# A product-key stage whose short lists move to PSUM and whose dense output is multiplied a quarter at a time

## The reference, cut to what matters

```python
q = (hidden_states @ Wq).reshape(b, t, 2, H, RET // 2)           # H = 4 heads
sim = jnp.einsum('btphn,hkpn->pbthk', q, keys)                   # 2 sides x 64 keys
sc, ix = jax.lax.top_k(sim, KPH)                                 # the 8 best of each side
all_sc = (sx[..., :, None] + sy[..., None, :]).reshape(b, t, H, KPH * KPH)
scores, pk = jax.lax.top_k(all_sc, KPH)                          # the 8 best of the 64 sums
w = silu(hidden_states . down_embed[idx]) * softmax(scores)
experts_states = sum over heads and k of w * up_embed[idx]
mlp = jax.nn.silu(hidden_states @ Wg + bg) * (hidden_states @ Wu + bu) @ Wd + bd
return mlp + experts_states
```

## Time and profile before

| | |
|---|---|
| median of 3 runs | 1288.74 us (1287.62 to 1289.69) |
| the profiled execution: its time | 1287.9 us |
| its span (first to last instruction) | 1286.1 us |
| mean granted clock of PE | 0.914 |
| busy: PE, DVE, ACT, POOL | 80%, 73%, 48%, 28% of the span |
| this stage | about 608 to 923 us of the span |

### The profile page before, as it was taken

One profiled execution on the slowest core, in us unless ns is written; L12 is line 12 of the kernel. 1 busy time (PEld: TensorE's weight loads), 2 busy tenths in 40 slices (PEclk: granted clock), 3 DMA queues, 4 the chain that ended last, 5 costly groups with the idle time before them and its releaser, 6 DMA issues.

```text
span 1286.1 us, 21270 instructions
## 1 busy us (share of the span) xinstructions
PE 1024.6 (80%) x7331; PEld 662.8 (52%) x7331; DVE 943.0 (73%) x2271; ACT 616.2 (48%) x958; POOL 361.8 (28%) x339
## 2 busy tenths in 40 slices
PE   5868500878969987996598888897879969999998
PEld 3653200844547753553166565576645446666665
DVE  4686699778866666777798889887468856666666
ACT  3424566366622336652565556664276523333332
POOL 5600000011200024451887788775002100000000
PEclk8889955989989999999599889998999979999999
DMA  7000000100000000000000000000000000000000
GB/s 261 1 1 1 1 0 0 59 4 2 2 2 1 0 1 1 2 1 1 1 1 1 1 0 0 0 0 1 1 2 2 2 1 9 9 8 8 8 9 17
DMA packets 8956, 13.47 MB, mean 10 GB/s; under 512 B 816, under 2 KB 6704, under 8 KB 8624
## 3 DMA queue, kind: packets, MB, share of 16 engines
q1 hardware_dynamic: 8880, 12.46, 2.8%
HBM read 10.36 MB, written 2.10 MB: 10 GB/s over the span
## 4 chain that ended last, share of the span: by engine, by line
PE 45%; DVE 34%; issue 12%; ACT 6%; POOL 2%; DVEq 1%; DMA 0%; SPq 0%; POOLq 0%; ACTq 0%
DVE big L718 6%; DVE big L713 6%; PE psum L1879 5%; PE psum L511 5%; PE psum L1882 5%; PE psum L1893 5%; PE psum L1574 3%; DVE big L1785 2%; PE psum L1366 2%; PE psum L1319 2%; DVE tmp L1750 2%; PE psum L1328 2%; ACT psum L1642 2%; PE psum L252 2%; DVE amax L1129 2%
## 5 line engine op out<-in xcount | busy, mean ns | idle before, releaser
L713 DVE TENSOR_REDUCE big<-psum 128x16 f32<-128x1024 f32 x96 | 114.4, 1221 | 70.9 <-PE psum L465 38.0
L1699 POOL TENSOR_TENSOR big<-big 128x512 f32<-128x512 f32 x128 | 134.7, 1086 | 19.9 <-ACT big L1622 19.9
L1929 ACT ACTIVATE big<-psum 128x512 f32<-128x512 f32 x80 | 47.8, 598 | 143.3 <-PE psum L1879 143.1
L1642 ACT ACTIVATE psum<-big,tmp 128x512 f32<-128x512 f32 x128 | 84.9, 687 | 37.2 <-DVE big L1785 33.3
L383 POOL TENSOR_TENSOR big<-big,w_const 128x256 f32<-128x256 f32 x48 | 34.7, 724 | 229.8 <-PE psum L511 216.0
L1785 DVE SCALAR_TENSOR_TENSOR big<-big,tmp,psum 128x512 f32<-128x512 f32 x128 | 90.3, 743 | 4.8 <-ACT psum L1642 1.8
L1709 POOL TENSOR_TENSOR big<-big 128x1024 f32<-128x1024 f32 x32 | 75.4, 2366 | 64.0 <-DVE big L1785 64.0
L1982 DVE TENSOR_TENSOR big<-big,psum 128x512 f32<-128x512 f32 x80 | 54.4, 687 | 53.1 <-PE psum L1882 52.9
L718 DVE RECIPROCAL big<-psum 128x256 f32<-128x256 f32 x48 | 83.9, 1749 | 11.8 <-PE psum L511 11.8
L1893 PEld LDWEIGHTS psum<-tmp,big 128*128 128x128 f32 x512 | 66.7, 191 | 40.0 <-issue 36.3
L619 ACT ACTIVATE big<-psum 128x1024 f32<-128x1024 f32 x64 | 62.0, 1021 | 51.3 <-PE psum L495 51.3
(11 more groups left out here) (239 smaller groups left out, 2391.2 us busy)
## 6 DMA issues: line engine op xcount, KB each, us to landing
out<-X SPq DMA_DIRECT2D x8, 256.0 KB, 2.3
tmp<-in_pack_f SPq DMA_DIRECT2D x1, 1924.0 KB, 7.8
w_f<-in_pack_f SPq DMA_DIRECT2D x1, 1280.0 KB, 12.3
tmp<-in_pack_once SPq DMA_DIRECT2D x1, 960.0 KB, 7.5
X<-in_x SPq DMA_DIRECT2D x1, 768.0 KB, 5.3
w_a<-in_pack_a SPq DMA_DIRECT2D x3, 256.0 KB, 7.6
w_a<-in_pack_a SPq DMA_DIRECT2D x1, 704.0 KB, 9.7
w_f<-in_pack_f SPq DMA_DIRECT2D x1, 576.0 KB, 5.0
```

Of the source, the lines that this page charges most:

```text
L713: dve.tensor_reduce(nm, psum[:, 1 + 2 * t:3 + 2 * t, :].rearrange("p c (r l k) -> p (c r) l k", r=2, k=SK), AX.X, ALU.max, negate=True).th ...
L1642: act.activation(bank(EX_BANK + h % 2), ssum[t][:, h * 512:(h + 1) * 512], ACT.Exp, bias=shift2[:, t * NH2 + h:t * NH2 + h + 1]).then_inc( ...
L1699: ins = pool.tensor_tensor(ssum[t][:, h * 512:(h + 1) * 512].rearrange("p (i j) -> p i j", i=ROWS2), st[:, 0, h, 0:ROWS2].unsqueeze(2).to_ ...
```

## The change

The dense output is split in four calls `dense_out(g, c)`, one quarter of the contraction each: quarters 0 and 1 follow the up product of c = 2 and 3, quarters 2 and 3 the transposes of group g+2. `total(g)` moves from behind the gates into them (after c = 1) and is two instructions instead of three. One of the two lists of eight (`top2y`), the eight best sums (`lead2`) and the sum of the weights (`tot2`) are put in PSUM banks 1 and 2, which the exponentials use later. ACT copies `lead2` to SBUF (`best2`) for the threshold that `weigh` reads, and DVE waits for that copy before the first `weigh`.

```diff
-        top2 = small(GT * 8 * 8).rearrange("p (t c k) -> p t c k", t=GT, c=8)
+        top2x = small(GT * 4 * 8).rearrange("p (t c k) -> p t c k", t=GT, c=4)
...
+        top2y = bank(1)[:, 0:128].rearrange("p (t c k) -> p t c k", t=GT, c=4)
+        lead2 = bank(2)[:, 0:128].rearrange("p (t h k) -> p t h k", t=GT, h=NH2)
+        tot2 = bank(2)[:, 128:128 + GT]
...
+            def dense_out(g, c):
+
+                if c == 0:
+                    pe.wait_ge(sem(s, "res"), at(s, "res") + g + 1)
+                pe.wait_ge(S("f2_aT"), 4 * g + c + 1 + 1)
+                for t in range(GT):
+                    pe.matmul(bank(7)[:, t * P:(t + 1) * P], aT[:, c, t * P:(t + 1) * P],
+                              W["f2_wd"][:, c * P:(c + 1) * P], start=(t == 0 and c == 0), stop=False,
+                              skip_group_check=True)
...
+                    if c >= 2:
+                        dense_out(g, c - 2)
                 if two_more:
                     T(g + 2, j)
-                pe.wait_ge(sem(s, "res"), at(s, "res") + g + 1)
-                pe.wait_ge(S("f2_aT"), 4 * g + 4 + 1)
-                for t in range(GT):
-                    for c in range(4):
-                        pe.matmul(bank(7)[:, t * P:(t + 1) * P], aT[:, c, t * P:(t + 1) * P],
...
+                dense_out(g, 2)
+                dense_out(g, 3)
 
                 def turn_weights(t):
 
-                    pe.wait_ge(S("f2_tt"), 3 * g + 3)
+                    pe.wait_ge(S("f2_tt"), 2 * g + 2)
...
+                if not (isinstance(G, int) and G == 0):
+                    act.wait_ge(S("f2_mw"), 16 * G)
+                act.activation(best2, lead2, ACT.Copy).then_inc(S("f2_b2"), 1)
...
             def top(G, t):
 
                 dve.wait_ge(S("f2_sim"), 4 * G + t + 1 + 2)
+                if t == 0 and not (isinstance(G, int) and G == 0):
+                    dve.wait_ge(S("f2_mw"), 16 * G)
                 settle(dve)
                 for c in range(8):
-                    dve.max(top2[:, t, c, :], sim[:, t * 512 + c * 64:t * 512 + (c + 1) * 64])\
+                    dve.max(top2x[:, t, c, :] if c < 4 else top2y[:, t, c - 4, :], sim[:, t * 512 + c * 64:t * 512 + (c + 1) * 64])\
                         .then_inc(S("f2_t1"), 1)
                 dve.wait_ge(S("f2_t1"), 32 * G + 8 * t + 8)
                 dve.tensor_tensor(pair2[:, t].rearrange("p h (a b) -> p h a b", a=8),
-                                  top2[:, t, 0:4, :].unsqueeze(3).to_broadcast([P, NH2, 8, 8]),
-                                  top2[:, t, 4:8, :].unsqueeze(2).to_broadcast([P, NH2, 8, 8]), ALU.add)\
+                                  top2x[:, t, :, :].unsqueeze(3).to_broadcast([P, NH2, 8, 8]),
+                                  top2y[:, t, :, :].unsqueeze(2).to_broadcast([P, NH2, 8, 8]), ALU.add)\
                     .then_inc(S("f2_t2"), 1)
...
                 for h in range(NH2):
-                    dve.max(best2[:, t, h, :], pair2[:, t, h, :]).then_inc(S("f2_t3"), 1)
+                    dve.max(lead2[:, t, h, :], pair2[:, t, h, :]).then_inc(S("f2_t3"), 1)
...
-                dve.tensor_tensor(e8, best2, best2[:, :, :, 0:1].to_broadcast([P, GT, NH2, 8]), ALU.subtract)\
+                dve.tensor_tensor(e8, lead2, pair2[:, :, :, 0:1].to_broadcast([P, GT, NH2, 8]), ALU.subtract)\
...
-                dve.scalar_tensor_tensor(out=shift2.rearrange("p (t h) -> p t h", t=GT), in0=best2[:, :, :, 0],
+                dve.scalar_tensor_tensor(out=shift2.rearrange("p (t h) -> p t h", t=GT), in0=lead2[:, :, :, 0],
...
             def weigh(G, t):
 
+                if t == 0:
+                    dve.wait_ge(S("f2_b2"), G + 1)
                 for h in range(NH2):
...
-                                             accum_out=tots2[:, t * NH2 + h:t * NH2 + h + 1])\
+                                             accum_out=tots2[:, t, h:h + 1])\
...
-                dve.tensor_reduce(tot2, tots2.rearrange("p (t h) -> p t h", t=GT), AX.X, ALU.add)\
+                dve.tensor_reduce(tot2, tots2, AX.X, ALU.add).then_inc(S("f2_tt"), 1)
+                dve.wait_ge(S("f2_fold"), 4 * G + 4)
+                dve.wait_ge(S("f2_tt"), 2 * G + 1)
+                last_col = ew_v[:, :, NEXP2 - 1]
+                dve.scalar_tensor_tensor(out=last_col, in0=tot2, scalar=-1.0, in1=last_col, op0=ALU.mult, op1=ALU.add)\
                     .then_inc(S("f2_tt"), 1)
-                dve.wait_ge(S("f2_tt"), 3 * G + 1)
-                dve.tensor_scalar(tot2, tot2, -1.0, float(NH2), ALU.mult, ALU.add).then_inc(S("f2_tt"), 1)
-                dve.wait_ge(S("f2_fold"), 4 * G + 4)
-                dve.wait_ge(S("f2_tt"), 3 * G + 2)
-                last_col = ew_v[:, :, NEXP2 - 1]
-                dve.tensor_tensor(last_col, last_col, tot2, ALU.add).then_inc(S("f2_tt"), 1)
-
+
+            dve.memset(tots2[:, :, NH2], -float(NH2)).then_inc(S("f2_tz"), 1)
...
+                    if c == 1:
+                        total(g)
                 if one_more:
                     less_best(g + 1)
-                total(g)
-                if one_more:
                     z(g + 1)
                     shift(g + 1)
```

More of the change, by code:

```diff
@@ L1523, in build @@
         e8 = small(GT * 4 * 8).rearrange("p (t h k) -> p t h k", t=GT, h=NH2)
-        z2, lnz2, shift2, tots2 = (small(GT * NH2) for _ in range(4))
-        tot2 = small(GT)
+        z2, lnz2, shift2 = (small(GT * NH2) for _ in range(3))
+        tots2 = small(GT * (NH2 + 1)).rearrange("p (t h) -> p t h", t=GT)
         EX_BANK = 1
+        top2y = bank(1)[:, 0:128].rearrange("p (t c k) -> p t c k", t=GT, c=4)
+        lead2 = bank(2)[:, 0:128].rearrange("p (t h k) -> p t h k", t=GT, h=NH2)
+        tot2 = bank(2)[:, 128:128 + GT]
         NFOLD = 2
@@ L1567, in body @@
                         .then_inc(S("f2_u_ps"), 1)
+                    if c >= 2:
+                        dense_out(g, c - 2)
                 if two_more:
                     T(g + 2, j)
-                pe.wait_ge(sem(s, "res"), at(s, "res") + g + 1)
-                pe.wait_ge(S("f2_aT"), 4 * g + 4 + 1)
-                for t in range(GT):
-                    for c in range(4):
-                        pe.matmul(bank(7)[:, t * P:(t + 1) * P], aT[:, c, t * P:(t + 1) * P],
-                                  W["f2_wd"][:, c * P:(c + 1) * P], start=(t == 0 and c == 0), stop=False,
-                                  skip_group_check=True)
+                dense_out(g, 2)
+                dense_out(g, 3)
                 def turn_weights(t):
-                    pe.wait_ge(S("f2_tt"), 3 * g + 3)
+                    pe.wait_ge(S("f2_tt"), 2 * g + 2)
                     for c in range(4):
```

## The result

The changed kernel takes 1240.27 us (median of 4 runs, 1239.75 to 1241.70) against 1288.38 for the kernel before in the same comparison; the ratio is 0.9627, with a 95% interval of 0.9611 to 0.9644. The profiled execution took 1240.38 us, with a span (first to last instruction) of 1238.6. The forecast was 1244, with a range of 1237 to 1258.

The account below looks back on a forecast made before the run. PE waiting for DVE's last `aT`, then running at low clock, was taken as the bound. Idle 30.3, clock 13.0 and start 2.0 us make 45.3, less shape changes 44.5: 1244 us forecast, range 1237 to 1258.

Parts of the forecast that it names:

- The clock's part: PE's dense products: time beyond 3.83 us in each of eight groups, lost to the lower clock, goes: 13.0 us.
- The pair sum: DVE in the gates: with one operand in PSUM it takes 0.43 us, against 0.96 in the middle before.
- the step from one `aT` to the next: DVE in the gates: the pitch falls from 3.18 to 2.65 us.
- the start: Before the first group: the chain through the last pair sum, `less_best` and `shift` gets 2.0 us shorter.
- Writes to PSUM: DVE's lists: a write costs nothing extra, with 0.06 us per instruction as the upper bound.
- Rival 1: DVE's PSUM writes are dearer: at 0.06 us, 28 MAX8 cost 1.7 us per group, total 1249; 15%.
- The spare time on DVE: Before quarter 3: DVE's last `aT` is done 0.9 us early, so PE never waits.
- changes of shape: On PE: three more per group from splitting the dense output, 0.1 us per group taken off the gain.
- Rival 2: PE's last two quarters and turning stay at 1.2 GHz: 21 us back, total 1265; 7%.
- Rivals 3, 4 and 5: 3: DVE keeps waiting for POOL, 1258, 5%; 4: MAX8 stalls writing PSUM, 1299, 2%; 5: turning waits elsewhere, unchanged, 1%.

Follow-up runs that it names:

- the repeat: The changed kernel run and profiled once more as a control, nothing changed: 1240.32 us, ratio 0.9643.
- lists alone: Changed kernel with the dense output back in one piece behind the gates and `total` behind `less_best`, `tot2` in bank 1: 1261.50 us against 1287.94 before.
- quarters alone: The kernel before with its dense output in four quarters, `total` and all lists as before: 1284.36 us against 1287.94, ratio 0.9969.

## Why the prediction was right

**The bound.** It was read rightly: PE waits for the last `aT`, then runs at half clock. The earlier trace rows carried the sum, and the same row of the profile after has 0.2 us of idle time where 30.3 was to go. The clock's part, 13.0 us in the sum, was measured by itself with PE kept busy.

**DVE beside POOL.** The pair sum was set at 0.43 and is 0.42; `less_best` at 0.3 and is 0.29; the step from one `aT` to the next at 2.65 and is 2.66; the start at 2.0 and is 2.14. That POOL is what stretches these instructions was argued from L722 and L1837, and is shown by the kernel without POOL's sums.

**Writes to PSUM.** Between zero and 0.06 us the prediction took zero: 9 ns was measured, 218 against 209. Rival 1 falls. The Trainium skill's 125 against 60 ns (Perfetto Trace Analysis, "Optimizing Scalar/DVE Operations") is not what this trace shows: neither a source in PSUM (421 ns against the 426 of the fastest from SBUF) nor a destination there (9 ns) costs DVE anything like 65 ns.

**The spare time on DVE** was set at 0.9 us. In the trace it is less: in the group before the one shown, the last `aT` ends at 714.53 and quarter 3 can start at about 714.8, half of the 1.95 us behind 713.87. In the group shown it is 743.62 against 744.3. It was enough, but rival 1 at its bound would have cost more than was said. Part of the good fit is therefore luck: the price of a write was chosen, not known, and at 0.06 us for each of 28 MAX8 PE would have waited in every group.

**The total.** The sum was 3.5 us too small. None of the 0.8 us for changes of shape was paid: four quarters take 3.57 us from start to start in the changed kernel, the 16 products in one piece took 3.64 in the last group of the kernel before. Six groups gained 1.0 more than foreseen; this was not traced further. Group 0 gained 0.8 more, for PE came to full clock sooner: its first three products of 512 columns took 1.91, 1.92 and 1.41 us before and 1.91, 1.15 and 1.02 after. The last group gained 0.8 more in this profile and 1.8 in the repeat; as seen above, what it takes hangs on the clock at its opening, which no term of the sum had.

**Rival 2**, the clock staying low, did not come: 1.00 through the steady groups. But it was nearer than its 7%. The argument against it, that the clock "only fell in groups with 4.5 us of idle time", was a misreading of the kernel before: in its last group, after 2.29 us, the products at 892.18 took 2.07 us where they take 1.16 at full clock. The lists alone show the same for 2 us, and quarters alone that a wait moved to another place takes the clock loss with it. **Rivals 3, 4 and 5** fall with the rows above. What the prediction did not see is how much the two halves need each other. Asked for each half alone, the same reasoning gave 19 us for the quarters, where 3.6 came.

## What to carry to other kernels

When a long wait on PE is followed by products that last longer than elsewhere, the wait costs twice; price both, and when you shorten a wait in part, ask whether what is left still takes the clock down, for half a cure can bring a tenth of the gain. An instruction of DVE with operands in SBUF that has several durations while POOL runs may be waiting inside its busy time, as here; one operand moved to PSUM, even to a bank that is only free for now, ended that here at 9 ns for each MAX8. Take a mean over the groups as the base of a sum, not the group whose timeline you happen to have on the screen. And when two kernels differ by a few us, compare them first in the part that was changed: here the unchanged rest moved by up to 3 us from run to run.

## What the runs showed of the hardware that was not expected

- Products whose results nobody reads made two kernels faster: the kernel before by 11.9 us (1288.32 to 1276.43), and the quarters alone by some 5.6 us (9.2 us below its before with them, 3.6 without).
- After about 2 us of idle time PE's next products were sometimes at full clock and sometimes not, in one and the same kernel: 3.84 us after 2.02 us, 5.47 us after 1.99 us. After the 2.29 us before the last group it was so in nine profiles of 13.
- A DVE instruction of four elements took 1.19 us beside POOL and 0.17 without it, and the profile shows no idle time for the difference.
- POOL gained too: its 128 sums took 134.7 us before and 128.7 after, though nothing in them was changed.
- With nothing changed in it, the next stage took 120.3 to 121.4 us where the clock in its first 29 us was 1.00 or 0.94, and 122.4 to 123.4 where it was 0.88 or 0.82 (13 profiles). One and the same kernel took 122.4 and 121.2, with 0.82 and 1.00. Gains of 2 to 4 us in the stage before were hidden by this and by the last group.
